# Step tables of their own for the last two rows of a fused selective-scan and FFN kernel

## The reference, cut to what matters

```
xx, res = split(x @ in_w.T)              # 512 inner channels each
xx = silu(causal_conv4(xx) + conv_b)
delta, B, C = split(xx @ xproj_w.T);  delta = softplus(delta @ dt_w.T + dt_b)
h[l] = exp(delta*A)*h[l-1] + delta*B*xx  # 512 channels x 16 states, over 512 positions
y = sum_n h*C + xx*D;  y = y * silu(res)
x1 = layernorm(x + y @ out_w.T)
h = silu(x1@w1*s1) * (x1@w2*s2);  h = gelu(h@h1*s);  h = gelu(h@h2*s)   # 1024 hidden
out = layernorm(x1 + (h@w3)*s)
```

## Time and profile before

| what | us |
|---|---|
| median of 3 runs (2790.53 to 2793.53) | 2791.72 |
| the profiled execution | 2790.6 |
| its span, first to last instruction | 2788.8 |
| PE busy | 2443.8 (88%) |
| DVE busy | 2435.8 (87%) |
| ACT busy | 2106.6 (76%) |
| POOL busy | 1623.6 (58%) |

### The profile page before, as it was taken

How to read it: one execution, slowest core, us unless ns; L and a number is a source line. 1 busy time by engine, 2 the same in 40 slices (tenths; PEclk the granted TensorE clock), 3 DMA queues, 4 the chain that set the end, 5 groups by cost and what they waited for, 6 DMA issues and landing times. The chain is left out here.

```text
span 2788.8 us, 36144 instructions
## 1 busy us (share of the span) xinstructions
PE 2443.8 (88%) x12034; PEld 1850.7 (66%) x12034; DVE 2435.8 (87%) x2402; ACT 2106.6 (76%) x3205; POOL 1623.6 (58%) x1572
## 2 busy tenths in 40 slices
PE   4466998989899898989989898998989999898988
PEld 2335675766767576676757667675766767576767
DVE  7798899899999989998998999999898999989730
ACT  5576887969788796978969697896969789696711
POOL 1224755665675666567566656756665576666544
PEclk6568999999999999999999999999999999999999
DMA  7968898988889898888989889898988889898933
GB/s 263 268 131 178 202 223 199 234 208 211 211 208 223 201 233 208 208 210 210 224 203 230 210 208 212 206 225 204 230 208 205 209 213 227 201 229 203 241 108 117
DMA packets 226798, 581.68 MB, mean 209 GB/s; under 512 B 25920, under 2 KB 26304, under 8 KB 226128
## 3 DMA queue, kind: packets, MB, share of 16 engines
q0 software_dynamic: 73728, 268.47, 52.1%
q1 hardware_dynamic: 152880, 310.84, 33.3%
HBM read 301.86 MB, written 20.45 MB: 116 GB/s over the span
## 5 line engine op out<-in xcount | busy, mean ns | idle before, releaser
L770 DVE TENSOR_TENSOR_SCAN scan_ps<-dA,scan_ps 128x1024 f32<-128x1024 f32 x416 | 951.9, 2288 | 127.4 <-PE scan_ps L408 112.4
L977 POOL DMA_DIRECT2D y<-hC x512 | 449.3, 878 | 695.7 <-DVE hC L781 547.0
L635 ACT ACTIVATE dB<-duT,bT 128x512 f32<-128x512 f32 x1024 | 715.1, 711 | 131.5 <-PE scan_ps L408 131.5
L408 PE MATMUL scan_ps<-ident,dB 128*128 128x128 f32 x4096 | 578.2, 288 | 150.3 <-DVE hC L781 124.6
L626 ACT ACTIVATE dA<-delta,a_neg 128x512 f32<-128x512 f32 (+1 forms) x1024 | 692.3, 711 | 1.1
L521 PE MATMUL ffn_ps<-hb_hi,ring 128*128 128x512 f32 x1536 | 654.5, 426 | 36.6 <-POOL hb_lo L1016 20.0
L408 PEld LDWEIGHTS scan_ps<-ident,dB 128*128 128x128 f32 x4096 | 499.8, 148 | 266.8 <-DVE hC L781 103.2
L521 PE MATMUL ffn_ps<-hb_lo,ring 128*128 128x512 f32 x1536 | 611.9, 398 | 0.0
L781 DVE TENSOR_TENSOR hC<-scan_ps,c_rows_sb 128x1024 f32<-128x1024 f32 x416 | 507.2, 1219 | 38.4 <-DMA c_rows_sb<-c_rows 8.2
L521 PE MATMUL ffn_ps<-ha_hi,ring 128*128 128x512 f32 x1024 | 437.1, 427 | 7.4 <-POOL ha_lo L1016 4.6
L521 PE MATMUL ffn_ps<-ha_lo,ring 128*128 128x512 f32 x1024 | 402.0, 393 | 0.0
(11 more groups left out here) (99 smaller groups left out, 3161.2 us busy)
## 6 DMA issues: line engine op xcount, KB each, us to landing
y<-hC POOLq DMA_DIRECT2D x512, 512.0 KB, 5.9
ring<-rounded_weights SPq DMA_DIRECT2D x704, 256.0 KB, 4.1
c_rows_sb<-c_rows SPq DMA_DIRECT2D x256, 256.0 KB, 4.6
x<-ffn_w SPq DMA_DIRECT2D x22, 512.0 KB, 6.8
rounded_weights<-ffn_w SPq DMA_DIRECT2D x22, 512.0 KB, 9.0
xt<-x_chan SPq DMA_DIRECT2D x16, 512.0 KB, 3.9
xt<-x_tok SPq DMA_DIRECT2D x16, 512.0 KB, 4.8
out_st<-x_chan SPq DMA_DIRECT2D x16, 512.0 KB, 4.2
```

Source lines behind the costliest of these rows:

```text
L408: mm = nc.tensor.transpose(dst[:, j * P:(j + 1) * P], src(j), ident[:])
L635: nc.scalar.activation(dB[:, n % 2, t, :], duT[:, t, :], ACT.Copy, scale=bT2[:, par, t, n:n + 1]).then_inc(dB_ready, 1)
L770: nc.vector.tensor_tensor_scan(states, dA[:, a:a + 2, :].rearrange("p a l -> p (a l)"), b, 0.0, ALU.mult, ALU.add).then_inc(scan_done, 1)
L977: pool.dma_start(y2[:, par, c:c + 2, :], hC[:, slot], accum_op=ALU.add).then_inc(y_added[p % 2], 16)
```

## The change

The step tables are put into named tuples, one for most rows (`STEADY`, the same numbers as before), one for row 14 (`NEXT_TO_LAST`), one for row 15 (`LAST`), and `steps(r)` chooses. All engines now also walk `tail_step(scan, s - TILES)`, so a negative position is a step of the row's own scan iteration.

- Row 14: the 32 half tiles, until now on steps 31 to 71, stand on steps 29 to 63 (iteration 15); Gelus and splits with them; w3 on 65 to 68 in place of 74 to 78; norm at 88 in place of 86, store at 90 in place of 88.
- Row 15: the gate products stand on steps 35, 36, 37 and 40 of iteration 15 in place of 0, 4, 5 and 8 of iteration 16, tanh and v on 35, 37, 39, 43. The four gates are kept in `du`, which is free there, and are multiplied into `y2` all at step 1 of iteration 16, on DVE (`gate_tile`, waiting as POOL's did for the last adds into `y2`). Its x is loaded at step 28 in place of 51.
- The first ring entries of row 15 are asked for at step 4 of iteration 16 in place of step 14.

```diff
+T_MUL = (3, 6, 8, 12)
-E_W3 = (10, 11, 13, 14)
+E_W3 = (74, 75, 77, 78)
...
+N_HALF_AT = (29, 30, 31, 32, 34, 35, 36, 37, 38, 39, 40, 42, 43, 44, 45, 46, 47, 48, 50, 51, 52, 53, 54, 55, 56, 57,
+             58, 59, 60, 61, 62, 63)
+N_GELU_AT = (32, 33, 39, 39, 43, 44, 45, 45, 51, 54, 54, 56, 58, 59, 60, 62)
+N_SPLIT_AT = (32, 41, 42, 44, 45, 46, 47, 47, 50, 51, 52, 55, 58, 62, 63, 63)
+N_W3 = (65, 65, 66, 68)
+N_SCALE = (66, 73)
+N_ADD = (73, 78)
+N_STATS = (76, 85)
+N_NORM = 88
+N_OUT_AT = 90
+L_XR = 28
+L_RES = (-29, -28, -27, -24)
+L_GATE = (-29, -27, -25, -21)
+L_MUL = (1, 1, 1, 1)
...
+def steps(r):
+
+    return LAST if r == BATCH - 1 else NEXT_TO_LAST if r == BATCH - 2 else STEADY
...
+        def gate_of(r, c):
+
+            return du[:, c, :] if r == BATCH - 1 else gate[:, c % 2, :]
...
-                    if s == OUT_AT and end is not None:
+                    if end is not None and s + TILES == steps(end).out_at:
...
-                    if s == F_XR and 0 <= i < BATCH:
+                    if s == (L_XR if i == BATCH - 1 else F_XR) and 0 <= i < BATCH:
                         load_res(i, front, end)
...
                     if tail is not None:
                         tail_step(tail, tpar, s)
+                    if scan is not None:
+                        tail_step(scan, spar, s - TILES)
...
+            def gate_tile(r, par, c):
+                if c == 0:
+                    for k in range(2):
+                        dve.wait_ge(y_added[k], r * (8 * PAIRS) + 8 * PAIRS)
+                dve.wait_ge(v_ready, r * DC + (c + 1))
+                nc.vector.tensor_tensor(y2[:, par, c, :], y2[:, par, c, :], gate_of(r, c), ALU.mult).then_inc(y_gated, 1)
```

More of the change, by code:

```diff
@@ L1 @@
+from collections import namedtuple
 from contextlib import ExitStack
@@ L57 @@
 SPLIT_AT = (40, 42, 43, 48, 48, 49, 51, 52, 59, 59, 61, 66, 66, 67, 72, 73)
+N_HALF_AT = (29, 30, 31, 32, 34, 35, 36, 37, 38, 39, 40, 42, 43, 44, 45, 46, 47, 48, 50, 51, 52, 53, 54, 55, 56, 57,
[12 more added lines that the diff above has]
+L_MUL = (1, 1, 1, 1)
+Steps = namedtuple("Steps", "res gate mul out add stats norm x1t l1 l1_split half gelu split w3 scale z2 z2_stats z2_norm out_at")
+STEADY = Steps(T_RES, T_GATE, T_MUL, T_OUT, T_ADD, T_STATS, T_NORM, T_X1T, L1_AT, L1_SPLIT_AT, HALF_AT, GELU_AT, SPLIT_AT,
+               E_W3, E_SCALE, E_ADD, E_STATS, E_NORM, OUT_AT)
+NEXT_TO_LAST = STEADY._replace(half=N_HALF_AT, gelu=N_GELU_AT, split=N_SPLIT_AT, w3=N_W3, scale=N_SCALE, z2=N_ADD,
+                               z2_stats=N_STATS, z2_norm=N_NORM, out_at=N_OUT_AT)
+LAST = STEADY._replace(res=L_RES, gate=L_GATE, mul=L_MUL)
+def steps(r):
+    return LAST if r == BATCH - 1 else NEXT_TO_LAST if r == BATCH - 2 else STEADY
 F_XX = (30, 32, 34, 36)
@@ L86 @@
 LOW_BITS = 0xFFFF
-X_FRONT_AT, OUT_AT = 22, 24
+X_FRONT_AT = 22
 X32 = 4
@@ L358, in iteration @@
                             load_c(front, 0)
[L359 to L362, removed]
+                    for f, at in ((end, s + TILES), (tail, s), (scan, s - TILES)):
+                        if f is not None:
+                            load_weights(f, [e for e in range(entry_count(full)) if entry_step(f, e, full) == at], full)
                     if s == X_FRONT_AT and front is not None and tail is not None:
@@ L476, in tail_step @@
             def tail_step(r, par, s):
-                if s in T_RES:
-                    c = T_RES.index(s)
+                if s in steps(r).res:
+                    c = steps(r).res.index(s)
                     if c:
@@ L498, in tail_step @@
                     mm.then_inc(pe_out, 1)
-                if s in T_X1T:
-                    k = T_X1T.index(s)
+                if s in steps(r).x1t:
+                    k = steps(r).x1t.index(s)
                     if k:
@@ L576, in iteration @@
             def iteration(i, par, full):
-                (scan, _), (front, fpar), (tail, tpar), (end, _) = rows(i, par)
+                (scan, spar), (front, fpar), (tail, tpar), (end, _) = rows(i, par)
                 for s in range(TILES):
@@ L588, in iteration @@
                                          ).then_inc(low_total, 1)
-                    if end is not None and s in E_W3:
-                        w3_tile(end, E_W3.index(s), full)
+                    for f, at in ((end, s + TILES), (tail, s)):
+                        if f is not None:
+                            for t in range(len(steps(f).w3)):
+                                if steps(f).w3[t] == at:
+                                    w3_tile(f, t, full)
                     if tail is not None:
                         tail_step(tail, tpar, s)
+                    if scan is not None:
+                        tail_step(scan, spar, s - TILES)
                     if front is not None:
                         front_step(i, front, fpar, s, tail)
-                    if end is not None:
-                        if s + TILES in HALF_AT:
-                            half_tile(end, HALF_AT.index(s + TILES), full)
+                    if end is not None and s + TILES in steps(end).half:
+                        half_tile(end, steps(end).half.index(s + TILES), full)
                     if tail is not None:
[L599 to L602, removed]
+                        if s in steps(tail).l1:
+                            l1_tile(tail, steps(tail).l1.index(s), full)
+                        if s in steps(tail).half:
+                            half_tile(tail, steps(tail).half.index(s), full)
             iteration(-1, 1, False)
@@ L683, in tail_step @@
             def tail_step(r, s):
-                if s in T_GATE:
-                    c = T_GATE.index(s)
+                if s in steps(r).gate:
+                    c = steps(r).gate.index(s)
                     act.wait_ge(pe_res, r * DC + (c + 1))
-                    if c >= 2:
+                    if c >= 2 and r < BATCH - 1:
                         act.wait_ge(y_gated, r * DC + (c - 1))
-                    nc.scalar.activation(gate[:, c % 2, :], misc_ps[:], ACT.Tanh).then_inc(v_tanh, 1)
-                if s in T_X1T:
-                    k = T_X1T.index(s)
+                    nc.scalar.activation(gate_of(r, c), misc_ps[:], ACT.Tanh).then_inc(v_tanh, 1)
+                if s in steps(r).x1t:
+                    k = steps(r).x1t.index(s)
                     act.wait_ge(pe_x1T, r * KD + (k + 1))
@@ L709, in ffn_step @@
                 for i in range(2 * HC):
-                    if GELU_AT[i] == s:
+                    if steps(f).gelu[i] == s:
                         gelu_tile(f, i)
@@ L723, in iteration @@
                             step(front, fpar, tile - TILES)
+                    if scan is not None:
+                        tail_step(scan, s - TILES)
                     if tail is not None:
@@ L861, in tail_step @@
             def tail_step(r, par, s):
-                if s in T_GATE:
-                    c = T_GATE.index(s)
+                if s in steps(r).gate:
+                    c = steps(r).gate.index(s)
                     dve.wait_ge(v_tanh, r * DC + (c + 1))
-                    nc.vector.scalar_tensor_tensor(out=gate[:, c % 2, :], in0=gate[:, c % 2, :], scalar=1.0,
+                    nc.vector.scalar_tensor_tensor(out=gate_of(r, c), in0=gate_of(r, c), scalar=1.0,
                                                    in1=misc_ps[:], op0=ALU.add, op1=ALU.mult).then_inc(v_ready, 1)
-                if s in T_ADD:
-                    k = T_ADD.index(s)
+                if r == BATCH - 1:
+                    for c in range(DC):
+                        if steps(r).mul[c] == s:
+                            gate_tile(r, par, c)
+                if s in steps(r).add:
+                    k = steps(r).add.index(s)
                     dve.wait_ge(pe_out, r * TT + (2 * k + 2))
@@ L930, in iteration @@
             def iteration(i, par):
-                (scan, _), (front, fpar), (tail, tpar), (end, epar) = rows(i, par)
+                (scan, spar), (front, fpar), (tail, tpar), (end, epar) = rows(i, par)
                 for s in range(TILES):
@@ L938, in iteration @@
                     if end is not None:
-                        end_step(end, epar, s)
+                        end_step(end, epar, s + TILES)
                     if tail is not None:
                         tail_step(tail, tpar, s)
+                    if scan is not None:
+                        tail_step(scan, spar, s - TILES)
                     if front is not None:
                         front_step(front, fpar, s, tail)
-                    if tail is not None and s in L1_AT:
-                        l1_tile(tail, L1_AT.index(s))
+                    if tail is not None and s in steps(tail).l1:
+                        l1_tile(tail, steps(tail).l1.index(s))
                     if i * TILES + s - 1 in PREP_AT:
@@ L1019, in ffn_step @@
             def ffn_step(f, s):
-                if s in L1_SPLIT_AT:
-                    split_tile(f, L1_SPLIT_AT.index(s))
```

(12 more changed lines are left out.)

51 lines of the change are left out of this document (26 added, 25 removed).

## The result

The changed kernel took 2796.88 us (median of 16 runs) beside 2790.96 us of the kernel before (16 runs): ratio 1.0022, 95% interval 1.0015 to 1.0029. The forecast was 2789.7. The profiled execution has a span of 2794.6 us, 5.8 more than before.

What follows compares the result with a forecast made beforehand. PE's work was taken to set the end after 2649, with 10.1 us lost ahead of it. Terms -2.3 (half 1 to H), -0.3 (H to first L1 tile) and +0.6 (norm) gave -2.0 us: 2789.7, range 2784.8 to 2795.5.

Steps and rivals of the forecast that it cites:

- Half 1 to H: PE from row 14's half tile 1 to H: idle time filled, H 2.3 us earlier, at 2663.5.
- H: The point where row 14's last half tile ends on PE: 2665.8 before, forecast 2663.5.
- Waits for weights: PE's remaining waits for weights between half tile 1 and H: 2.0 us, bounds 0 and 7.
- the split of half 17: PE's wait at half tile 17 for the eighth Gelu and its split: 0.8 us, bounds 0 to 2.
- the moved load of 512 KB: Load moved to step 28, around 2568, where PE waits for splits anyhow: taken as hidden.
- the pair's 0.79: PE time of pair 17, which falls behind half tile 1: one transposed pair more before H, 0.79 us.
- the first tanh: Gates in row 15's scans: DVE late by some 3 us at step 35, with slack; cost 0, bounds 0 and 3.
- H to the first L1 tile: w3, projection and the chain to row 15's first L1 tile: -0.3 us, between -0.5 and +0.1.
- Norm at step 88: Row 14's norm on DVE between row 15's second and third L1 tiles: costs 0.6 us, 0 to 1.4.
- The multiplications into y2: Four on DVE after the last add lands at H + 4, ending by H + 9: barely hidden behind w3.
- Rival B: In the scans, more function table switches make ACT the bound: +5.1 us, 2796.8; chance 0.13.

Runs made afterwards that it cites:

- e9: e5 with row 14's half tiles 1, 2 and 3 on steps 32, 32 and 33, so pair 17 is transposed before half 1: ratio 0.9987 to the kernel before.
- e10: e9 with only w3 tile 0 ahead of row 15's projection and tiles 1 to 3 behind it: ratio 0.9990 to the kernel before.
- e6: Changed kernel with row 14's tables of before, norm and store too; only row 15's gates are moved: ratio 0.9999 to the kernel before.
- e2: Changed kernel with five of row 14's splits moved behind their Gelus on POOL: ratio 1.0010 to the kernel before.
- e3: Changed kernel with both edits, row 14's norm at 86 (e1) and the five later splits (e2): ratio 1.0004 to the kernel before.
- e1: Changed kernel with row 14's norm back at step 86, its store still at 90: ratio 1.0011 to the kernel before.
- e4: Kernel before with only row 14's norm at step 88 and its store at 90: ratio 1.0003 to the kernel before.
- e8: Changed kernel with Tanh in place of Gelu for row 14, so 19 function table loads go: ratio 1.0012 to the kernel before.
- e5: e2 with w3 tiles 2 and 3 behind row 15's projection and row 14's end behind the last L1 tile: ratio 0.9988 to the kernel before.

## Why the prediction was wrong

*Half 1 to H: right.* Half 1 started behind POOL, pair 17 followed, and H came 82.0 us behind half 1 (forecast 2.3 us less than before, measured 2.9 less). Waits for weights were 0.7 us (2.0 taken), the split of half 17 cost 0.7 (0.8). One wait I had not reckoned: 1.07 us at 2653.92, for the product that DVE made late for want of a buffer. PE waits for no weights behind the moved load of 512 KB. e9 and e10 agree with the pair's 0.79. DVE stood 4.6 us for the first tanh (some 3 reckoned), and e6 shows no cost of it to PE.

*H to the first L1 tile: the step that failed.* I took w3 from the last row, "9.4 us from the last half to its end", and put the part at -0.3. Measured: +4.3 - 0.4. The last row has nothing beside it on POOL and DMA; here two things arrive later. The split of the last Gelu stands on POOL behind adds that were held up by splits listed ahead of their Gelus (e2: 1.4 us in the profile, some 3 in the runs), and the last weights can be asked for only at H (e3: a wait of 2.9 us). In the changed kernel the low clock behind PE's wait cost 1.3 us more in w3; behind e3's wait of 2.88 us it didn't fall.

The order of POOL could have been read from the two tables: `N_SPLIT_AT` has split 9 at 51 where `N_GELU_AT` has its Gelu at 54, and of every wait one has to ask what is queued behind it. I did that for DVE at the gates and not for POOL.

*Norm at step 88: mechanism right, size wrong.* Taken as 0.6 (0 to 1.4). Measured: a wait of PE of 1.6 to 1.9 us in all five profiles with the norm there, and in four of them some 1.7 more at 1.2 GHz behind it, 1.6 to 3.6 in all. The runs agree without telling more: 3 us less in e1, and 0.8 us more in e4 with an interval up to 3.3. I had bounded the term by the instructions' own 1.39 us, and they took 2.70 beside POOL's split. The Trainium skill ("SBUF — State Buffer", section "Who interferes with whom") says that `tensor_scalar` on VectorE in a two-port mode and GpSimd take a shared pair of ports in turn, and whoever comes second stands for the whole instruction. The five norms beside a split took 2.70 and the seven beside none 1.38 or 1.39, a difference of 1.31 where the subtraction takes 1.27; this agrees, though no run took POOL's work away from beside a norm at step 88, and no row says in which mode the four instructions ran.

*The multiplications into y2: hidden, as forecast, but later.* They started at H + 7.5 in the changed kernel (forecast H + 4), ended at H + 10.0, and w3 still hid them (to H + 13.8). Without the late adds it is H + 4.1 to 6.6 (e3).

*Rival B gave almost the measured time, 2796.8, for a reason that the runs refute.* The switches are 19, as counted, and ACT was busy 70.2 us. But DVE never waited for `dA` in that stretch, and H was early: ACT didn't set the pace of the scans. The switches did matter, by making Gelus late for POOL: without them (e8) the wait for the last split is gone too. So B had the right suspect and the wrong path, and that its sum met the measured time is luck. The 0.13 that I gave to slower was too little: I had priced each moved part by its own work, and each of the two losses was in what stood behind it.

*The last 1.6 us stay open.* Row 15's dense part takes 57.7 or 59.1 to 59.4 us, in different kernels with nearly the same wait ahead of it (2.26 before: 57.7; 2.24 in e1: 59.3). The slow ones run their first matmuls at 1.2 GHz. The granted clock there is 1.00 before (2712.98 to 2718.00), 0.57 in the changed kernel (2717.10 to 2721.10) and 0.63 in e1 (2716.40 to 2721.00). One profile each can't say whether it is chance or follows from the time of arrival.

## What to carry to other kernels

When work is moved along a list that engines walk in order, lay the tables of producer and consumer side by side: a consumer that stands ahead of its producer holds up everything queued behind it, here the adds that free another engine's buffers. Work that leaves a shadow can cost more than its own time: a norm of 1.4 us put between tiles made TensorE wait 1.6 to 1.9 us and mostly run slowly behind it. And where two chains end together, put first only what the longer one waits for. With both faults mended, the moves of the change gained nothing over the kernel before (e3); with w3's second part in TensorE's idle gap and row 14's end behind the L1 tiles they gained 3 us (e5).

## What the runs showed of the hardware

The clock often was low behind a short wait of TensorE, but the length of the wait didn't decide it. The granted clock was 0.50 in 2663 to 2668 of e9 behind a wait of 2.81 us and 0.70 in 2666 to 2670 of e5 behind 3.00; it stayed at 1.00 behind 2.88 in e3, behind 2.26 in the kernel before (at 2712.98) and behind 1.57 in e4. Behind 1.85 us in the changed kernel (at 2703.30) it was 0.57 for the next 4 us. The rows are those of e9, e3 and the kernel before:

```profile
2663.00:2668.00 5.00, 5.00 (x23) 5.00 (x24) 2.23 (x4) 0.00 (x0) 0.00 (x0) 0.50 0.01 2
...
2663.60:2668.60 5.00, 5.00 (x42) 5.00 (x42) 2.94 (x5) 0.00 (x0) 0.00 (x0) 1.00 0.01 2
...
2712.98:2718.00 5.02, 5.02 (x22) 4.18 (x23) 0.00 (x0) 0.69 (x1) 1.90 (x2) 1.00 0.20 58
```

Four `tensor_scalar` on DVE, 1.39 us together, took 1.31 us more beside one GpSimd subtraction of 1.27 us.
